# A graph layer on one core: 8 more tiles in the head, 18 instead of 11 fetched by SyncE, layernorm factors in PSUM, and an epilogue without ScalarE

## The reference

```python
h = relu(layernorm(x))                       # x: 12500 nodes x 64
W = einsum('rb,bio->rio', comp, basis)       # 64 relations, each 64 x 64
msg = h[src] * edge_weight                   # 200000 edges, sorted by dst
s = segment_sum(msg, etype * N + dst, R * N) # sums by relation and node
agg = relu(einsum('rni,rio->no', s, W) + bias)
y = agg + relu(h @ res_w.T + res_b)
out = x + (y - mean(y)) * rsqrt(var(y) + eps) * gamma + beta   # mean, var over nodes
```

## Time and profile before

| | us |
|---|---|
| median of three runs | 1999.26 |
| profiled execution | 2000.53 |
| its span, first to last instruction | 1998.4 |
| PE busy (matmuls) | 1633.6 |
| POOL busy | 1497.1 |
| DVE busy | 929.6 |
| ACT busy | 902.4 |

### The profile page before, as it was taken

The page is one execution under the profiler, slowest core; times in us unless marked ns, Lnnn a source line. Parts: engine busy times, 40 slices in busy tenths (PEclk is TensorE's granted clock), DMA queues, the critical chain, the costliest instruction groups (busy, mean ns, idle before and its releaser), DMA issues. The chain is left out here.

```text
span 1998.4 us, 29426 instructions
## 1 busy us (share of the span) xinstructions
PE 1633.6 (82%) x6559; PEld 820.3 (41%) x6559; DVE 929.6 (47%) x3234; ACT 902.4 (45%) x2186; POOL 1497.1 (75%) x1570
## 2 busy tenths in 40 slices
PE   4599999999999869988889898998998889716444
PEld 4244444433333246555545553553543434212223
DVE  6631111311110069877746773873856848215223
ACT  4587777777777465544415442442424333001001
POOL 6777777777777777777777777777777777777774
PEclk9999999999999655555575557558577787857555
DMA  9599999999999522222211221221211211122112
GB/s 180 203 402 404 405 405 402 406 405 404 406 401 406 184 48 54 48 49 49 49 38 43 49 49 28 53 49 31 47 39 37 48 32 37 33 59 55 27 26 79
DMA packets 118340, 308.13 MB, mean 154 GB/s; under 512 B 47016, under 2 KB 47267, under 8 KB 92846
## 3 DMA queue, kind: packets, MB, share of 16 engines
q1 hardware_dynamic: 57830, 236.59, 30.3%
q0 software_dynamic: 49664, 50.96, 12.7%
q10 hardware_dynamic: 10672, 18.68, 3.2%
HBM read 80.01 MB, written 226.09 MB: 153 GB/s over the span
## 5 line engine op out<-in xcount | busy, mean ns | idle before, releaser
L546 POOL DMA_INDIRECT shared<-z_table,idx_all x1032 | 988.7, 958 | 316.1 <-issue 248.1
L519 POOL DMA_INDIRECT acc<-in_x,idx_all x520 | 503.6, 968 | 163.0 <-issue 157.9
L1133 PE MATMUL zps<-wp,res 128*128 128x512 bf16 x2352 | 531.9, 382 | 35.2 <-ACT zst L580 26.4
L580 ACT ACTIVATE zst<-zps 128x512 f32<-128x512 f32 (+1 forms) x784 | 411.5, 602 | 149.2 <-DMA z_table<-zst 127.8
L1133 PEld LDWEIGHTS zps<-wp,res 128*128 128x128 bf16 x2352 | 219.1, 98 | 338.4 <-ACT zst L580 98.1
L1260 PE MATMUL mps<-res 128*128 128x160 f32 (+4 forms) x694 | 344.5, 600 | 3.4 <-issue 2.7
L1010 DVE TENSOR_SCALAR shared<-iota,rel_all,wgt_all 128x36 f32<-128x36 f32 (+10 forms) x1043 | 315.6, 329 | 1.0 <-issue 0.8
L1246 PE MATMUL aps<-shared 128*64 128x36 f32 (+10 forms) x1040 | 206.8, 314 | 126.0 <-DMA shared<-z_table,idx_all 66.0
L1246 PE MATMUL zps<-shared 128*64 128x36 f32 (+10 forms) x1024 | 204.9, 312 | 107.9 <-DMA shared<-z_table,idx_all 63.2
L690 ACT ACTIVATE res<-res,hw 128x64 f32<-128x64 f32 x520 | 175.1, 337 | 201.8 <-DVE hw L1036 131.8
L1246 PEld LDWEIGHTS aps<-shared 128*64 128x64 f32 x1040 | 133.1, 191 | 323.6 <-issue 154.3
(11 more groups left out here) (170 smaller groups left out, 934.1 us busy)
## 6 DMA issues: line engine op xcount, KB each, us to landing
z_table<-zst SPq DMA_DIRECT2D x194, 1024.0 KB, 9.8
wp<-z_table SPq DMA_DIRECT2D x1408, 0.2 KB
head_rows<-acc SPq DMA_DIRECT2D x65, 256.0 KB, 9.7
shared<-z_table,idx_all POOLq DMA_INDIRECT x1032, 2.5
res<-head_rows ACTq DMA_DIRECT2D x63, 256.0 KB, 2.8
acc<-in_x,idx_all POOLq DMA_INDIRECT x520, 6.4
zst<-in_x SPq DMA_DIRECT2D x12, 256.0 KB
out_x<-zst SPq DMA_DIRECT2D x12, 256.0 KB
```

The source lines that it names most:

```text
L519: e.indirect_dma_start(out=ring[:, b % NRING, i, :], out_offset=None, in_=x, in_offset=bass.IndirectOffsetOnAxis(ap=idx_all[:, t:t + 1], a ...
L546: e.indirect_dma_start(out=ys[:, q % NY, :], out_offset=None, in_=table[:, :], in_offset=bass.IndirectOffsetOnAxis(ap=idx_all[:, col:col + ...
L580: e.activation(to, frm, ACT.Copy).then_inc(s_ez, 1)
L1133: last = e.matmul(to, lhsT=stationary(px, pw), rhs=moving(px, pw), start=(a == 0), stop=(a == 2))
```

## The change

Five things change.

- The head is 528 tiles instead of 520, so the table serves 1035. `HEAD_ENDS`, the windows (`WINS`, each now for 13 groups of 8 tiles) and the end of the head's items in `sums` move with it.
- `SP_EVERY` is 50 instead of 80. The rule then gives SP 18 tiles instead of 11: 151, 207, 255, 303, and so on to 1023.
- The means of x and the reciprocals of its deviations are written to, and read from, bank 1 of `aps` in PSUM.
- The node sums `acc` are not cleared to 0 but begun at the bias in the lower 64 partitions (`bias_low`), and ACT's `shifted` is gone: DVE takes the sum from PSUM, does relu and the addition in one instruction.
- The last transposes go through 6 banks instead of 4 (`final_psum`). PE's sum of chunk n waits for DVE's sum (`s_ey`) of chunk n - 4 where it waited for ACT's shift (`s_eh`).

```diff
-HEAD, MAIN = 520, 512
+HEAD, MAIN = 528, 512
-HEAD_ENDS = (212, 301, 368, 425, 475, HEAD)
+HEAD_ENDS = (215, 304, 373, 431, 482, HEAD)
-WIN_BLOCK = 12
-WINS = (36, 42, 46, 50, 54, 60, 64, 70, 72, 78, 82)
+WIN_BLOCK = 13
+WINS = (36, 42, 48, 52, 56, 62, 66, 72, 78, 82)
-SP_EVERY, SP_FIRST, NSP = 80, 150, 3
+SP_EVERY, SP_FIRST, NSP = 50, 150, 3
...
+        xmean, xfac = (aps[:, 1, k * NT:(k + 1) * NT] for k in range(2))
...
+        def final_psum(n):
+            return (zps[:, 0, :], zps[:, 1, :], zps[:, 2, :], zps[:, 3, :], aps[:, 0, :], aps[:, 1, :])[n % NFP]
...
-            def shifted(n):
-                w = epi_width[n]
-                e.wait_ge(s_e1, n + 1)
-                e.activation(acc[:, n * EPI:n * EPI + w], halves_psum(n)[:, 0:w], ACT.Relu, bias=cols[:, 0:1]).then_inc(s_eh, 1)
...
-                    clear(acc[:, a:min(a + 2048, ARENA)]).then_inc(s_acc, 1)
+                    clear(acc[:, a:min(a + 2048, ARENA)], ACT.Identity, bias=bias_low[:, :]).then_inc(s_acc, 1)
...
-                link(e.tensor_scalar(mom[:, 1, t0:t1], mom[:, 0, t0:t1], 1.0 / F, None, ALU.mult))
+                link(e.tensor_scalar(xmean[:, t0:t1], mom[:, 0, t0:t1], 1.0 / F, None, ALU.mult))
                 e.tensor_tensor(xr[:, t0:t1, :], xr[:, t0:t1, :],
-                                mom[:, 1, t0:t1].unsqueeze(2).broadcast_to([P, LNT, F]), ALU.subtract).then_inc(s_xc, 1)
+                                xmean[:, t0:t1].unsqueeze(2).broadcast_to([P, LNT, F]), ALU.subtract).then_inc(s_xc, 1)
...
-                e.reciprocal(mom[:, 3, t0:t1], mom[:, 3, t0:t1]).then_inc(s_ln, 1)
+                e.reciprocal(xfac[:, t0:t1], mom[:, 2, t0:t1]).then_inc(s_ln, 1)
...
-                                mom[:, 3, t0:t1].unsqueeze(2).unsqueeze(3).broadcast_to([P, t1 - t0, 2, F]),
+                                xfac[:, t0:t1].unsqueeze(2).unsqueeze(3).broadcast_to([P, t1 - t0, 2, F]),
...
-                e.wait_ge(s_eh, n + 1)
-                e.tensor_tensor(y, y, res[:, n, 0:w], ALU.add).then_inc(s_ey, 1)
+                e.wait_ge(s_e1, n + 1)
+                e.scalar_tensor_tensor(out=y, in0=halves_psum(n)[:, 0:w], scalar=0.0, in1=res[:, n, 0:w],
+                                       op0=ALU.max, op1=ALU.add).then_inc(s_ey, 1)
...
+            e.tensor_copy(bias_low[0:F, :], cols[0:F, 0:1]).then_inc(s_low, 1)
+            e.memset(bias_low[F:P, :], 0.0).then_inc(s_low, 1)
...
                 if n >= NZB:
-                    e.wait_ge(s_eh, n - NZB + 1)
+                    e.wait_ge(s_ey, n - NZB + 1)
...
-                if n >= NZB:
-                    e.wait_ge(s_oc, n - NZB + 1)
+                if n >= NFP:
+                    e.wait_ge(s_oc, n - NFP + 1)
```

More of the change, by code:

```diff
@@ L25 @@
 NOH = 20
+NFP = 6
 UT = 4
@@ L83, in rgcn_kernel @@
     assert LE < UT * P and 2 * UT * P == GE and GB == 65
-    assert 64 < GB <= GA <= P and HEAD % GT == 0 and HEAD % HB == 0 and HR <= P and 0 <= len(WINS) * WIN_BLOCK - NGZ < WIN_BLOCK
+    assert 64 < GB <= GA <= P and HEAD % GT == 0 and HEAD % HB == 0 and HR <= P and len(WINS) * WIN_BLOCK == NGZ
     NU = GT // UT
@@ L216, in rgcn_kernel @@
         sacc = zflat[:, 0:SUM_NODES * HALF]
-        mom = sb("mom", [P, 4, NT])
+        mom = sb("mom", [P, 3, NT])
         idx_all = sb("idx_all", [P, NG * GT], I32)
@@ L252, in rgcn_kernel @@
         cols = sb("cols", [P, 4])
+        bias_low = sb("bias_low", [P, 1])
         gstat = sb("gstat", [P, 2, 3, NU])
@@ L306, in rgcn_kernel @@
                ("ld", "fix", "me", "zero", "clr", "bcast", "row", "idx", "y", "mul", "mm", "sum", "add", "back", "tp", "tc", "go")}
-        s_e1, s_eh, s_ey, s_bst, s_st, s_sc, s_scp, s_o, s_oc, s_out = (
-            sem(n) for n in ("s_e1", "s_eh", "s_ey", "s_bst", "s_st", "s_sc", "s_scp", "s_o", "s_oc", "s_out"))
-        s_cols = sem("s_cols")
+        s_e1, s_ey, s_bst, s_st, s_sc, s_scp, s_o, s_oc, s_out = (
+            sem(n) for n in ("s_e1", "s_ey", "s_bst", "s_st", "s_sc", "s_scp", "s_o", "s_oc", "s_out"))
+        s_cols, s_low = sem("s_cols"), sem("s_low")
         AHEAD = 2
@@ L589, in deviation @@
                 e.wait_ge(s_var, c + 1)
-                e.activation(mom[:, 3, c * LNT:(c + 1) * LNT], mom[:, 2, c * LNT:(c + 1) * LNT], ACT.Sqrt).then_inc(s_dev, 1)
+                e.activation(mom[:, 2, c * LNT:(c + 1) * LNT], mom[:, 1, c * LNT:(c + 1) * LNT], ACT.Sqrt).then_inc(s_dev, 1)
             def first_part(n):
@@ L652, in _, with clear @@
                 e.activation(res[:, n, 0:w], bank_of(("r", n))[:, 0:w], ACT.Relu, bias=cols[:, 1:2]).then_inc(s_ez, 1)
-            def shifted(n):
-                w = epi_width[n]
-                e.wait_ge(s_e1, n + 1)
-                e.activation(acc[:, n * EPI:n * EPI + w], halves_psum(n)[:, 0:w], ACT.Relu, bias=cols[:, 0:1]).then_inc(s_eh, 1)
             flag = fast_path_flag(e)
             with e.If(flag >= 1):
-                def clear(to):
+                def clear(to, func=ACT.Copy, **bias):
                     w = to.shape[1]
-                    return e.activation(to, ones[:, 0:1].broadcast_to([P, w]), ACT.Copy, scale=0.0)
+                    return e.activation(to, ones[:, 0:1].broadcast_to([P, w]), func, scale=0.0, **bias)
                 head_stored(e)
                 e.wait_ge(s_me, len(METAS))
+                e.wait_ge(s_low, 2)
                 for a in range(0, ARENA, 2048):
-                    clear(acc[:, a:min(a + 2048, ARENA)]).then_inc(s_acc, 1)
+                    clear(acc[:, a:min(a + 2048, ARENA)], ACT.Identity, bias=bias_low[:, :]).then_inc(s_acc, 1)
                 table_landed(e)
@@ L699, in _ @@
                             clear(sacc[:, a:a + 2048]).then_inc(s_flush, 1)
[L700 to L707, removed]
             e.wait_ge(s_st, 4)
@@ L829, in stats_of_groups @@
                               mps[0:1, 0, 0:NU * NGZ].rearrange("p (h g) -> p h g", h=NU))
[L830 to L834, removed]
+                e.tensor_reduce(spans, mps[0:1, 1, 0:NU * NGZ].rearrange("p (h k g) -> p h k g", h=NU, g=WIN_BLOCK),
                                 AX, ALU.max).then_inc(s_me, 1)
@@ L1285, in _ @@
                     e.wait_ge(s_sc, n + 1 - pools)
-                if n >= NZB:
-                    e.wait_ge(s_oc, n - NZB + 1)
+                if n >= NFP:
+                    e.wait_ge(s_oc, n - NFP + 1)
                 for q in range(w // P):
-                    last = transpose(zps[:, n % NZB, q * P:(q + 1) * P], acc[:, n * EPI + q * P:n * EPI + (q + 1) * P], P)
+                    last = transpose(final_psum(n)[:, q * P:(q + 1) * P], acc[:, n * EPI + q * P:n * EPI + (q + 1) * P], P)
                 last.then_inc(s_o, 1)
```

12 lines of the change are left out of this document (7 added, 5 removed).

## The result

The changed kernel takes 1981.38 us (median of 4, 1980.18 to 1981.72) where the kernel before took 1999.6 beside it: ratio 0.9906, interval 0.9889 to 0.9923. Run a second time, it took 1981.37 against 2001.55: 0.9896, 0.9880 to 0.9913. Forecast were 1978.5 and a range of 1971 to 1990, so the time is 2.9 us above the forecast. Both hold on chips where the kernel before takes near 2000 us. On two others the kernel before takes 2606 and 2614 us. The change itself has no run there, but every kernel with its 18 fetched tiles is slower there than the kernel before, and rival C decides, as the experiments show.

The account below looks back on a forecast made before the run. Bound by the table's landing (about 671.3 us), GpSimd's 1032 gather periods and a 25.06 us tail. 2000.5 + 1.0 - 18.8 - 2.3 - 0.4 - 0.3 = 1979.7 profiled, less 1.27: 1978.5 us, range 1971 to 1990.

Parts of the forecast that it names:

- rival C: SP's row fetches become the bound above 71.3 us a tile (0.557 us a row), each further 1 us costing 18; chance 0.06.
- The head: Head gathers: operands in PSUM save 8.6 us, eight more tiles add 10.0; GpSimd through at 671.0 instead of 669.56.
- The row that it rested on: Head gathers beside L800, with one input in PSUM: 27 of 32 undisturbed, taken as the nearest row for the 8.6 us.
- The landing: End of the table's writing: additional bytes of 0.52 MB cost +1.0 us, bounds 0 to 1.3.
- 15 gathers fewer: Gathers of the table: GpSimd issues 1017 instead of 1032, each 1.251 us, -18.8 us.
- L928: Epilogue: DVE's sum takes its input from PSUM and stops disturbing 16 gathers, -2.3 us, bounds 0 to 2.3.
- the step to the median: End of the sum: 1.27 us taken off the profiled execution's time to get the median.
- The tail: From the last gather to the end: -0.4 us for ACT's part of the last chunk and -0.3 for six banks.
- The hop over ScalarE: Last chunk in the tail: loses ACT's 0.37 us and its handover, -0.4 us.
- The six banks: Last transposes in the tail: six banks instead of four cut DVE's waits for PE, -0.3 us, bounds 0 to -0.7.
- SP keeps up: Table gathers: SP fetches a tile in 62.6 us (0.489 us a row), one being wanted every 63.4 us.

Follow-up runs that it names:

- psum alone: Kernel before with only x's means and factors moved to PSUM, 11 fetched tiles: 2611.95 us, ratio 1.0021, on the 2606 us chip.
- head528 alone: Kernel before with only the head changed to 528 tiles, factors in SBUF: 2613.06 us, ratio 1.0005, on the 2606 us chip.
- fetch50 alone: Kernel before with only SP_EVERY at 50, so 18 fetched tiles: 2964.93 us (1.1374) on the 2606 us chip, 2962.04 us (1.1321) on the 2614 us chip.
- factors back: Changed kernel with x's means and factors back in SBUF: 1988.51 us (0.9932) beside 2000.94; on slow chips 2968.01 us (1.1363) and 2965.37 us (1.1340).

## Why the prediction was right, and what was off

**The head.** The mechanism was right and the first gather of the table only 0.8 us off. The row that it rested on was read nearly right: 34 gathers (not 32) overlap an L800 in the trace of before, 29 of them under 0.96 us. The disturbances fell from 12.7 to 5.5 us (sum over all head gathers of their length above 0.944), by 7.2 and not 8.6: the 38 gathers' 8.6 us went but for 0.3, while 528 gathers now lie elsewhere, and another line with two SBUF inputs (L789, ten gathers, 2.7 us; L795 before, nine, 1.3) took 1.4 us back. So GpSimd is through at 672.89 and not at 671.0.

**The landing** was forecast 1.0 us later for the additional bytes, and that term is neither confirmed nor refuted. Its last recorded event is at 670.38 in the one trace of before, at 670.28 and 672.85 in the two of the change, and between 668.5 and 673.5 in the other four kernels with 528 head tiles on such chips: the scatter is larger than the term. GpSimd and the table come within 3 us of each other, and either can be the last, as the two traces show.

**15 gathers fewer** were worth what they were to be: the table's part is 18.9 us shorter, and undoing 7 of them costs 8.0 us.

**L928 was worth 2.3 us and the total kept almost nothing of it.** Behind 1735 us the disturbances went from 2.5 to 0.2 us, as forecast. But between 660 and 1735 they rose from 11.9 to 14.0 us (13.4 in the second trace of the change, 12.4 with 11 tiles). The step that failed is that I held all other disturbances fixed. The subtract of the head rows (L1023, now L1020) has part in the rise: 79 gathers beside it were 8.1 us too long, 76 are now 9.1; what brings the rest is not shown. That any shift sets anew which gather meets which is the likely reason and no run separates it.

So the 2.9 us by which the forecast was low are, by the table above, +0.8 of the first gather, +2.2 of the table's part and -1.0 of the tail, 2.0 in all for the profiled execution (1981.72 against 1979.7). The other 0.9 lie in the step to the median: I took 1.27 us off, and here the profiled execution is 0.34 above its median.

**The tail** gave 1.7 us where I had 0.7. The hop over ScalarE is 0.45 of it. The six banks show no gain: the 13 additions span 8.7 us, 8.6 before, with waits of 0.16 as before; no run undoes them alone. The remaining 1.4 us lie between the last addition and the end, which I had at nothing: 5.7 us in the trace of before, 4.2 to 4.5 in the six of its successors on such chips, the one with the old epilogue too. Scatter isn't likely. On the slower chips the three traces with 520 head tiles have 5.5 to 5.7 us, and the four with 528 have 4.2 to 4.5. Here are the last additions of `psum alone` (span 2603.7) and of `head528 alone` (span 2601.6), which has the old epilogue, four banks and 11 tiles:

```profile
2592.27 5.67 DVE L1084 TENSOR_TENSOR zst<-zst,zps 128x512 f32<-128x512 f32 x10 [0.16 <-PE zps L1090]
```
```profile
2590.64 6.42 DVE L1083 TENSOR_TENSOR zst<-zst,zps 128x512 f32<-128x512 f32 x11 [0.16 <-PE zps L1089]
```

They end about 5.7 and 4.5 us before the span does. So in 14 traces this part goes with the head's 528 tiles and with nothing else that was changed; why the last stores should be done sooner behind them, no run shows.

**SP keeps up** was right on the chips with 2000 us (0.492 us a row) and wrong on the others, and with it the weight of rival C: its threshold of 71.3 us a tile was passed by far. In `fetch50 alone` on the 2614 us chip SP spent 1915 us on 18 tiles (1019.6 to 2934.9), 106 us each, with at most 24 us of waits for PE among them, and the end came 30 us behind. I had priced C from a row pace that one trace of one chip showed.

Undone one by one on chips with near 2000 us, the parts cost 7.1 (operand), 8.0 (seven tiles) and 1.1 us (epilogue, below what can be told), 16.2 of the 18.2 to 20.2 us by which the change is ahead. The eight tiles of the head were not undone there. What is left has the size of two things in the traces: the pause before the table's first gather (1.80 us, now 0.30 and 1.02), which eight more head gathers fill in part or whole, and the end that is 1.4 us shorter.

## What to carry to other kernels

Where an engine issues gathers back to back and sets the end, its own price list is not enough: list which vector operations overlap it with two inputs in SBUF, since moving one input to PSUM, or the operation to another engine, can pay as much as several gathers less. Before work goes to a queue that is to be busy without a gap, work out the pace from which it would decide and what each step beyond costs, and look for that pace on more than one chip: here the same 18 tiles instead of 11 are worth 0.4% on one and cost 13% on two others. And where disturbances depend on who meets whom, taking one of them away can bring others: here 2.3 us went and 2.0 came. Leave such a term a few us of room in both directions.

## What the runs showed of the hardware

The place of one operand decides: a gather beside a product of 128x512 takes 0.94 us with the second input in PSUM and 1.41 with it in SBUF, beside a subtract of 128x896 0.94 and 1.64, three times over (before, change, factors back). The Trainium skill (GPSIMD Engine Reference, Specifications) has the contention for an instruction with two SBUF inputs; that broadcasting the PSUM operand (14 values over 896 columns) changes nothing about it is seen only here.

Unexpected was the difference between chips. One program took 1999 to 2002 us on some and 2606 to 2614 on others. A table gather takes nearly the same on both (956 to 959 ns on the first, 952 to 957 on the others, wherever VectorE centres the head rows), and so does the median issue of a row fetch (225 ns); the rows' pace (0.49 against 0.78 us) and the writing of the table (400 against 264 to 274 GB/s) aren't the same.
